# Scatters of a graph kernel: the low part of the next free slots joins the running counts

## The reference, cut to what matters

```python
edge_index = jnp.stack([src, dst])
x = _layernorm(x + _L0_gnn_ref(x, edge_weight1, ..., src, dst, edge_type_32), axis=-1)
x = _layernorm(x + _L1_gnn_ref(x, edge_index, edge_weight, ...), axis=-1)
x = _layernorm(x + _L2_gnn_ref(x, edge_index, ...), axis=-1)
x = _layernorm(x + _L3_gnn_ref(x, node_vec1, src, dst, edge_attr_4, edge_attr_10, ...), axis=-1)
...
agg = jax.ops.segment_sum(msg, dst, num_segments=N)
```

## Time and profile before

| | us |
|---|---|
| median of 3 runs | 11323.88 |
| lowest, highest | 11316.15, 11333.89 |
| profiled execution | 11423.42 |
| its span, first to last instruction | 11421.7 |

### The profile page before, as it was taken

How to read it: one execution, slowest core, us unless ns; L and a number is a source line. 1 busy time by engine, 2 the same in 40 slices (tenths; PEclk the granted TensorE clock), 3 DMA queues, 4 the chain that set the end, 5 groups by cost and what they waited for, 6 DMA issues and landing times. The chain is left out here.

```text
span 11421.7 us, 173435 instructions
## 1 busy us (share of the span) xinstructions
PE 7099.6 (62%) x35190; PEld 5300.1 (46%) x35190; DVE 5879.9 (51%) x20916; ACT 3126.7 (27%) x10511; POOL 6581.8 (58%) x6970
## 2 busy tenths in 40 slices
PE   5444444433383333358888767777577777788888
PEld 3222223333332323334444356666566666777777
DVE  5555543333333333345544456666566666677776
ACT  2111110000020000000000044444344444677776
POOL 3666666666515655656666566666466665455554
PEclk5555555555585555555555556666666656899999
DMA  3222223111151111111111111111111111211111
GB/s 99 72 69 69 72 73 80 46 45 44 42 227 44 44 44 42 44 45 46 46 46 45 45 48 49 49 48 49 44 48 48 48 48 43 75 41 41 41 41 40
DMA packets 312728, 637.47 MB, mean 56 GB/s; under 512 B 138402, under 2 KB 181541, under 8 KB 300200
## 3 DMA queue, kind: packets, MB, share of 16 engines
q0 software_dynamic: 222080, 416.54, 14.1%
q1 hardware_dynamic: 81444, 212.40, 5.4%
q10 hardware_dynamic: 8484, 1.48, 0.1%
HBM read 479.02 MB, written 150.90 MB: 55 GB/s over the span
## 5 line engine op out<-in xcount | busy, mean ns | idle before, releaser
L1185 POOL DMA_INDIRECT relsum_rows<-relation_table,tab_idx x1950 | 1842.2, 945 | 1422.7 <-issue 484.9
L1241 PE MATMUL relsum_sums<-relsum_hot,relsum_rows 128*128 128x128 f32 x3900 | 1109.3, 449 | 1452.5 <-issue 797.1
L1241 PEld LDWEIGHTS relsum_sums<-relsum_hot,relsum_rows 128*128 128x128 f32 x3900 | 915.6, 307 | 1638.9 <-issue 1600.7
L1053 POOL DMA_INDIRECT conv_rows<-tensor_table,src_idx x997 | 939.9, 943 | 750.9 <-PE conv_sums L2360 357.2
L1053 POOL DMA_INDIRECT gat2sum_rows<-gat_table,src_idx x997 | 942.8, 946 | 587.7 <-PE gat2sum_sums L1971 308.6
L1053 POOL DMA_INDIRECT gat1sum_rows<-gat_table,src_idx x997 | 941.6, 944 | 582.3 <-PE gat1sum_sums L1971 255.1
L717 POOL DMA_INDIRECT records<-sort_recs,place_rows x968 | 926.4, 957 | 595.0 <-DVE place_rows L235 325.1
L1185 POOL DMA_INDIRECT gcnsum_rows<-x_table,src_idx x985 | 935.0, 949 | 562.6 <-PE gcnsum_sums L1241 259.1
L1969 PE MATMUL gat1sum_sums<-gat1sum_hot,gat1sum_scaled 128*128 128x128 f32 x1994 | 686.1, 443 | 413.0 <-DVE gat1sum_scaled L1898 332.9
L1197 DVE TENSOR_SCALAR relsum_hot<-iota_row,dst_rel,w 128x128 f32<-128x128 f32 x1994 | 722.8, 365 | 423.5 <-issue 421.4
L1969 PE MATMUL gat2sum_sums<-gat2sum_hot,gat2sum_scaled 128*128 128x128 f32 x1994 | 671.5, 436 | 432.3 <-DVE gat2sum_scaled L1898 302.0
(11 more groups left out here) (410 smaller groups left out, 15931.9 us busy)
## 6 DMA issues: line engine op xcount, KB each, us to landing
relation_table<-table_row SPq DMA_DIRECT2D x30, 2048.0 KB, 6.3
relsum_rows_SP<-relation_table SPq DMA_DIRECT2D x2816, 0.5 KB
relsum_rows_ACT<-relation_table ACTq DMA_DIRECT2D x2816, 0.5 KB
relation_table<-sort_space SPq DMA_DIRECT2D x40, 1024.0 KB
relsum_rows<-relation_table,tab_idx POOLq DMA_INDIRECT x1950
place_lo_wide<-lo_rows SPq DMA_DIRECT2D x121, 256.0 KB
gcnsum_rows_SP<-x_table SPq DMA_DIRECT2D x1536, 0.5 KB
relation_table<-place_extra SPq DMA_DIRECT2D x20, 1024.0 KB
```

The lines of the kernel that those rows point to most:

```text
L1053: pool.indirect_dma_start(bufs[:, t % depth, :], None, table, bass.IndirectOffsetOnAxis(ap=idx[:, t:t + 1], axis=0)).then_inc(landed[t % l ...
L1185: pool.indirect_dma_start(rows[:, t % depth, :], None, table, bass.IndirectOffsetOnAxis(ap=idx[:, t:t + 1], axis=0)).then_inc(landed[t % d ...
L1241: pe.matmul(bank[:, 0:P], tile_rows, hot[:, t % HOTS, :], start=True, stop=True).then_inc(s["multiplied"], 1)
```

## The change

The low part of the base is no longer multiplied once for each column. Instead the running count `taken` of a batch begins with it: its first product is `low` with an identity matrix (a new f16 tile `ident`, which ACT makes once from the f32 one). So `taken_in`, which ACT copies for each column, now holds low part and counts together, and it is needed for column 0 as well: ACT makes eight copies a batch instead of seven. The product of the high part moves into the columns, ahead of the wait for the copy. The batch no longer ends with the sixteen products; `owned` is posted by the product with the copy in the last column.

The wait for `based` moves from the end of the batch into column 0. `find_base` computes the new base from `taken` and the high part alone, since the low part is already in `taken`. `added` counts nine posts a batch instead of eight.

```diff
@@ find_base
-                    dve.wait_ge(s["added"], b * SB)
-                    dve.tensor_tensor(new, taken[1 - j][:, 0:BLKS], old, ALU.add)
-                    dve.tensor_tensor(high[:, j, :], taken[1 - j][:, 0:BLKS], old, ALU.add)
+                    dve.wait_ge(s["added"], b * (SB + 1))
+                    dve.tensor_tensor(new, taken[1 - j][:, 0:BLKS], high[:, 1 - j, :], ALU.add)
+                    dve.tensor_tensor(high[:, j, :], taken[1 - j][:, 0:BLKS], high[:, 1 - j, :], ALU.add)
@@ PE
             turn_x(0)
+            pe.wait_ge(s["ident_made"], 1)
...
-                    if k:
-                        pe.wait_ge(s["taken_copied"], b * (SB - 1) + k)
-                        pe.matmul(own[j][:, k, 0:BLKS], hot_lo_t[:, j, k, :], taken_in[:, k % 2, :], start=False, stop=True,
-                                  skip_group_check=True)
-                    pe.matmul(taken[j][:, 0:BLKS], hot_lo[:, j, k, :], hot_hi[:, j, k, :], start=k == 0, stop=True,
+                    if k == 0:
+                        pe.wait_ge(s["based"], b + 1)
+                        pe.matmul(taken[j][:, 0:BLKS], ident[:, :], low[:, j, :], start=True, stop=True,
+                                  skip_group_check=True).then_inc(s["added"], 1)
+                    pe.matmul(own[j][:, k, 0:BLKS], hot_lo_t[:, j, k, :], high[:, j, :], start=False, stop=True,
+                              skip_group_check=True)
+                    pe.wait_ge(s["taken_copied"], b * SB + k + 1)
+                    mm = pe.matmul(own[j][:, k, 0:BLKS], hot_lo_t[:, j, k, :], taken_in[:, k % 2, :], start=False, stop=True,
+                                   skip_group_check=True)
+                    if k == SB - 1:
+                        mm.then_inc(s["owned"], 1)
+                    pe.matmul(taken[j][:, 0:BLKS], hot_lo[:, j, k, :], hot_hi[:, j, k, :], start=False, stop=True,
                               skip_group_check=True).then_inc(s["added"], 1)
                     if left and k in (2, 5):
                         make_table(left.pop(0))
-                pe.wait_ge(s["based"], b + 1)
-                for k in range(SB):
-                    for digit in (high, low):
-                        mm = pe.matmul(own[j][:, k, 0:BLKS], hot_lo_t[:, j, k, :], digit[:, j, :], start=False, stop=True,
-                                       skip_group_check=True)
-                mm.then_inc(s["owned"], 1)
@@ ACT
+            act.copy(ident[:, :], env.ident[:, :]).then_inc(s["ident_made"], 1)
...
-                for k in range(1, SB):
-                    act.wait_ge(s["added"], b * SB + k)
+                for k in range(SB):
+                    act.wait_ge(s["added"], b * (SB + 1) + k + 1)
                     act.copy(taken_in[:, k % 2, :], taken[b % 2][:, 0:BLKS]).then_inc(s["taken_copied"], 1)
```

More of the change, by code:

```diff
@@ L540, in place_edges @@
         taken_in = sb("taken_in", [P, 2, BLKS], F16)
+        ident = sb("ident", [P, P], F16)
         picked = sb("picked", [P, SB, BLKS], F32)
@@ L555, in place_edges @@
             "hot", "based", "added", "taken_copied", "owned", "rows_ready", "self_written", "x_turned", "x_ready",
-            "table_made", "table_out")}
+            "ident_made", "table_made", "table_out")}
         lo_in = [env.sig(f"place_lo_in{j}").sem for j in range(lo_bufs)]
```

## The result

The changed kernel takes **11507.07 us** (median of 3 runs, 11499.87 to 11521.37), the kernel before 11323.88: ratio 1.0163, 95% interval 1.014 to 1.0186. That is 183 us slower, where +57 was forecast and 11450 was the upper end of the range. The direction came out as forecast, the size did not. The profiled execution of the changed kernel is at its median, 11507.07 (span 11505.4).

A forecast was written before the change was run, and what follows sets the result against it. The prediction took the edge-record stage to be bound by a circle of waits between POOL's scatters and PE's held products. +0.47 us x 121 batches = +57 us on 11324 gave 11380 us, with an 8-in-10 range of 11230 to 11450.

The forecast's parts named there:

- The bound and the pace: Edge-record placing stage: a circle of waits, 12.54 us a batch, from eight scatters (9.8 us) plus POOL's standstill (2.75 us).
- PE's completions held while POOL issues: Sixteen base products ending a batch: something holds their completion while POOL scatters, most strongly when many products stand close together.
- PE's own circle, 8.0 to 8.8 us, hidden behind POOL: PE's batch grows 0.8 us, hidden under 10.1 us of scatters; as a rival 97 us slower, 11421, chance 0.05.
- The base between "owned" and the pick, 0.47 us: On DVE: making the new base now falls between "owned" and the pick, adding nearly 0.47 us to POOL's gap.
- I take +0.47 us, the value of an unchanged release.: Chosen cost per batch, assuming PE's release behind POOL stays as before: x 121 = +57 us.
- the batch around 800 us: Batch in the old profile: pick ahead of POOL's end, gap 0.51 us, columns held 2.6 us, then POOL waits 5.9 us.
- what is gained in one gap is taken back in the next: POOL's gaps: two batches together no shorter than two ordinary ones; used to limit the faster case to 0.2-0.7 us a batch.
- upper bound of 0.98 us a batch: POOL's gap: 0.47 us plus a column's step of 0.51 us if PE is released with its last column open; 11443.
- lower bound of 0.2 us: Low end of the forecast's own case, per batch: 24 us, 11348.
- Faster, because the burst was the trouble: Rival at the batch's end: six fewer held products save time, 0.2 to 0.7 us a batch, middle 11270; chance 0.31.
- No change, because POOL bounds the batch: Rival: PE less held in timed runs, POOL's 10.1 us of scatters bound both kernels; 11324 within 22 us, chance 0.27.
- The chances of 0.58 for no loss: Whole-kernel odds given to the rivals without loss: no change 0.27 and faster 0.31.

The follow-up runs named there:

- a_paced: Changed kernel, with POOL also waiting for the first three columns of the next batch before a batch's scatters: 9368.91 us, ratio 1.0001.
- a_mid4: Changed kernel, with POOL waiting after a batch's fourth scatter until PE has counted the whole next batch: 9363.88 us against 9360.72 for the kernel before.
- a_pickfirst: Changed kernel, with DVE picking the ended batch's slots before making the next base: 11320.47 us (one run) beside 11315.01 for the kernel before.
- b_wait0: Kernel before, with only PE's wait for the new base moved to column 1, all products as before: 9367.77 us against 9367.94, ratio 1.0001.

## Why the prediction was wrong

**The bound and the pace**: right. The stage is a circle of waits; POOL's scatters at 957 ns and its standing still make the pace, before and after.

**PE's completions held while POOL issues**: right as a mechanism, and now shown: 8.7 and 7.8 us a batch with the scatters put off, in the setting where they are 14.4 and 12.5 otherwise. "Most strongly when many products stand close together" holds for sixteen against ten or four.

**PE's own circle, 8.0 to 8.8 us, hidden behind POOL**: right. Measured 7.84 and 8.73. As a rival (11421) it played no part: it costs 105 us only where POOL doesn't issue at all.

**The base between "owned" and the pick, 0.47 us**: right in place and size (869.91 to the pick at 870.37 is 0.46 us), but it does not add to each batch as I had it. POOL has one gap in two batches, so by these rows the 0.46 us stand for about 0.23 us a batch, an estimate of 28 us in place of 57; no run measures it alone.

**The step that failed is "I take +0.47 us, the value of an unchanged release."** The release did change, and in kind, not by its amount. With "owned" on the last column instead of behind sixteen products, PE's batch is let go before POOL has stopped whenever PE had a quick start; POOL then runs two batches in one, and PE's next batch stands in the slow part but for two columns. I had named the pieces: the columns that may be held, and the batch around 800 us of the kernel before in which just this happens, a gap of 0.51 us and then one of 5.89. But I read it as a proof that "what is gained in one gap is taken back in the next". The two gaps are 6.4 us together, where two ordinary ones are 5.6, so the pair was already 0.8 us longer; and between 200 and 1660 us there are four such pairs, the longer gap being 5.9 to 6.9 us. I didn't ask whether the change would make that exception the rule. The sum to make was that of a pair: a run of 16 x 0.957 + 15 x 0.30 = 19.8 us, then PE's held batch to finish. Its price could be bounded from the same rows: the gap of 5.89 us there gives (19.8 + 5.9) / 2 = 12.9 us a batch, and a gap of 8.8, as measured since, 14.3. The upper bound of 0.98 us a batch had no such case in it, and the lower bound of 0.2 us has no working behind it: the one given comes to -0.37. That the sign was right is in good part luck, since the sum had another cause in it.

**The rivals.** Faster, because the burst was the trouble: wrong, and the reverse of it: the burst was what kept the kernel at 12.5. No change, because POOL bounds the batch: that is what a_paced and a_mid4 show in the free setting, and not what happens in the recorded one; I had named the condition rightly (PE held less), but for the wrong occasion. The chances of 0.58 for no loss were too high for a change that takes away what separates two engines' turns.

**What would show it.** I had asked for picks 13.0 us apart and a POOL wait of 3.3 us. Picks were 14.46 apart, the wait 8.8 us in every second batch. The base's first add does stand directly ahead of the pick, 0.46 us before it. PE's idle time did move, from the first column after the base products to later ones, but only in every second batch and to columns 2 to 4 of it (ACT's copies at 883.61, 887.87 and 894.22), not to columns 5 to 7.

**What stays open**: why PE is slowed by POOL's scatters in one setting and not in the other, with scatters of 957 ns and a granted clock of 0.50 (1.2 GHz) in both; whether it is POOL's issuing or the transfers that it starts, which no run separates; where exactly in a run of scatters it sets in (7.6 us after its start in the stretch shown, but sooner behind a short pause, see below); and whether a version exists that beats the kernel before in the held setting. Picking first equals it in total (11320 beside 11315, one run) and is 0.45 us a batch behind it by the picks.

## What to carry to other kernels

When one engine slows another while it works, the mean of a gap is the wrong unit: ask whether the slowed engine can now finish early enough for the other to start its next turn without a pause, and sum up two turns, not one. An exception in the trace of before (here a gap of 0.5 us followed by one of 5.9) is where to look: work out its price as if it were the rule. And products that seem superfluous may be what keeps two engines in turns; sixteen useless ones bought back most of the 1.6% here, four did not.

## What the runs showed of the hardware

- The same kernel took 9361 to 9369 us in some comparisons and 11291 to 11434 in others, on chips whose number doesn't separate the two. In this stage the durations hardly differ (a scatter 957 to 961 ns, the pick 0.40 us, a granted clock of 0.50); what differs is how long PE's counts take to reach ACT and DVE while POOL issues scatters. The layers behind it, in which POOL issues indirect DMAs as well, account for 1722 of the 2053 us between the two profiled executions.
- In the held setting (changed kernel, 872 to 895 us) a round trip PE to ACT and back takes 0.51 us for the first 7.6 us of a run of scatters; then ACT waits 2.7 to 4.1 us for each count, and it is quick again about 2 us after POOL has stopped. A pause of 0.8 us between two runs was too short: in a_pickfirst, in a run that began at 813.26 behind such a pause, ACT waited 1.27 us before its copy at 815.40 and 2.66 us before the one at 818.25.
- In the free setting 0.88 us more of PE's batch cost nothing under POOL's 10.0 us of scatters: b_wait0 took 9367.77 and a_paced, with the products of the change, 9368.91.
- In the held setting the delay is longer the more products stand together: from their issue, 5.1 to 7.1 us into a run of scatters, to the pick it is 0.7 us for four, 1.9 to 2.7 for ten and 3.9 to 5.5 for sixteen.
